# A Mamba-2 layer's chunk states: 32-bit products against three passes of 16-bit halves

## The reference, cut to what matters

```python
xdt = xc * dtc[..., None]
scores = einsum('bclhn,bcshn->bchls', Cc, Bc) * Lmat
Ydiag = einsum('bchls,bcshp->bclhp', scores, xdt)
decay_states = exp(cs[..., -1:] - cs)
states = einsum('bclhn,bchl,bclhp->bchpn', Bc, decay_states, xdt)   # the product that changes
new = carry * cd + st                                                # a recurrence over the chunks
Yoff = einsum('bclhn,bchpn,bchl->bclhp', Cc, prev, exp(cs))
y = (Ydiag + Yoff + x * D) * silu(gate); out = y * rsqrt(mean(y*y) + eps) * norm_w; out @ out_proj.T
```

## Time and profile before

| | |
|---|---|
| time before, median of 3 runs | 2475.66 us (2474.8 to 2475.94) |
| the profiled execution, its own time | 2476.66 us |
| span of its instructions | 2474.6 us |
| mean granted TensorE clock over the span | 0.984 of full speed |
| PE busy | 2373.2 us, 96% |
| DVE, ACT, POOL busy | 1791.4, 1591.7 and 1255.2 us |

### The profile page before, as it was taken

How to read it: one execution, slowest core, us unless ns; L and a number is a source line. 1 busy time by engine, 2 the same in 40 slices (tenths; PEclk the granted TensorE clock), 3 DMA queues, 4 the chain that set the end, 5 groups by cost and what they waited for, 6 DMA issues and landing times. The chain is left out here.

```text
span 2474.6 us, 48904 instructions
## 1 busy us (share of the span) xinstructions
PE 2373.2 (96%) x15424; PEld 1359.8 (55%) x15624; DVE 1791.4 (72%) x3234; ACT 1591.7 (64%) x3327; POOL 1255.2 (51%) x1002
## 2 busy tenths in 40 slices
PE   6999999999999999999999998789999999999897
PEld 3555555555555555555555555445555555555443
DVE  5677787787777777787777776577777777778522
ACT  7676776776776776776776775365556555656422
POOL 4465555555556556556556569443434343454223
PEclk8999999999999999999999999989999999999899
DMA  7343343343343343343343441320110110100000
GB/s 249 101 132 108 115 130 107 115 131 108 113 133 105 115 133 106 114 134 105 113 134 105 131 146 50 138 89 1 43 44 1 44 44 1 43 18 1 1 0 34
DMA packets 113827, 218.79 MB, mean 88 GB/s; under 512 B 9632, under 2 KB 43040, under 8 KB 111360
## 3 DMA queue, kind: packets, MB, share of 16 engines
q1 hardware_dynamic: 113536, 215.28, 27.0%
HBM read 212.10 MB, written 3.15 MB: 87 GB/s over the span
## 5 line engine op out<-in xcount | busy, mean ns | idle before, releaser
L989 ACT ACTIVATE E<-wq,cst 128x128 f32<-128x128 f32 x1024 | 311.7, 389 | 3.0 <-PEq L298 3.0
L256 DVE SCALAR_TENSOR_TENSOR xc<-bank,taps,xc 128x511 f32<-128x511 f32 (+2 forms) x384 | 284.9, 742 | 35.5 <-ACT xc L243 18.0
L1919 POOL TENSOR_TENSOR qT<-qT,qrot 128x512 f32<-128x512 f32 x64 | 81.2, 1269 | 370.1 <-DVE qrot L1809 370.1
L1282 POOL TENSOR_TENSOR acc<-acc,sq 128x512 f32<-128x512 f32 x112 | 173.1, 1545 | 183.3 <-ACT sq L1001 183.3
L1273 POOL TENSOR_TENSOR xw<-xt,wdec 128x384 f32<-128x384 f32 x128 | 106.4, 831 | 294.1 <-DVE xt L1124 150.7
L1166 DVE SCALAR_TENSOR_TENSOR u<-xc,D,bank 128x512 f32<-128x512 f32 x128 | 95.6, 747 | 205.8 <-PE bank L814 194.2
L1105 DVE TENSOR_TENSOR E<-E,cbm 128x1024 f32<-128x1024 f32 x128 | 242.8, 1897 | 0.8
L59 PE MATMUL bank<-xhi,wx 128*128 128x512 f16 x640 | 242.8, 379 | 0.0
L60 PE MATMUL bank<-xlo,wx 128*128 128x512 f16 x640 | 242.8, 379 | 0.0
L61 PE MATMUL bank<-xhi,wx 128*128 128x512 f16 x640 | 242.6, 379 | 0.0
L1268 POOL TENSOR_TENSOR ecs<-ecs,xcC 128x768 f32<-128x768 f32 x128 | 234.1, 1829 | 0.4 <-POOLq L298 0.4
(11 more groups left out here) (240 smaller groups left out, 6315.0 us busy)
## 6 DMA issues: line engine op xcount, KB each, us to landing
wq<-cs_rows SPq DMA_DIRECT2D x128, 512.0 KB, 4.1
ecs<-ecs_rows SPq DMA_DIRECT2D x128, 384.0 KB, 3.6
wx<-in_w_xbc SPq DMA_DIRECT2D x80, 256.0 KB, 2.7
wz<-in_w_z SPq DMA_DIRECT2D x64, 256.0 KB, 2.7
wo<-in_w_o SPq DMA_DIRECT2D x64, 256.0 KB, 4.0
wq<-in_wq SPq DMA_DIRECT2D x8, 1024.0 KB, 5.8
awo<-in_wo SPq DMA_DIRECT2D x8, 1024.0 KB, 5.0
wkv<-in_wkv SPq DMA_DIRECT2D x8, 512.0 KB, 3.9
```

What stands on the lines that cost most here:

```text
L256: self.nc.vector.scalar_tensor_tensor(out=dst[:, d:T], in0=self.k.bank[bank][:, 0:T - d], scalar=self.taps[:, bass.ds(g, 1), b, j, 3 - d:4 ...
L989: ins = nc.scalar.activation(E[t.i % 4][:, h, c], sc.csr[t.i % 2][:, h, c * P:(c + 1) * P], ACT.Relu, scale=-1.0, bias=head(sc.cst, t, c, h))
L1282: nc.gpsimd.tensor_tensor(acc[t.b][:], acc[t.b][:], sq[:], ALU.add).then_inc(acc_done, 1)
```

## The change

PE's chunk states are no longer three products of 32-bit words: each is three passes over 16-bit halves, in the same place of PE's list. The halves come from these places:

- `bt` becomes `bthi` (16-bit, written by ACT as before, with the semaphore `bt_hi`) and `btlo`, the remainder, a new instruction of DVE in slot i = 6 (`rest_of_B`, and once in the opening). PE's wait is now on DVE's semaphore.
- `xw` stays in 32 bits; its leading half is read in place by `lead`. Its remainder `xwlo` is a new instruction of POOL behind each `xw`. PE's wait is now on the semaphore of the remainder.
- On DVE `turned_x` moves from behind the third tap to ahead of it, wherever there are taps of x.
- On PE `turn_B` moves from behind `output` to ahead of it, in slot i = 6.

```diff
-        bt = [sb(f"bt{i}", [P, CH - 1, P]) for i in range(NB)]
+        bthi, btlo = ([sb(f"bt{n}{i}", [P, CH - 1, P], F16) for i in range(NB)] for n in ("hi", "lo"))
+        xwlo = [sb(f"xwlo{i}", [P, CH - 1, P], F16) for i in range(2)]
...
                 def states(t):
-                    pe.wait_ge(xw_done, t.n + 1)
+                    pe.wait_ge(xw_lo, t.n + 1)
                     pe.wait_ge(bt_done, t.u + 1)
                     for c in range(CH - 1):
-                        mm = nc.tensor.matmul(W[:, c * P:(c + 1) * P], bt[t.b][:, c], xw[t.i % 2][:, c], start=True, stop=True)
+                        mm = product(nc, W[:, c * P:(c + 1) * P], (bthi[t.b][:, c], btlo[t.b][:, c]),
+                                     (lead(xw[t.i % 2][:, c]), xwlo[t.i % 2][:, c]), True, True)
                     mm.then_inc(st_ready, 1)
...
+                    if nu and s.i == 6:
+                        turn_B(nu)
                     if tile_at(g, m - 1):
                         for half in range(2):
                             output(tile_at(g, m - 1), half)
                     if nu and s.i == 5:
                         products_CB(nu)
-                    if nu and s.i == 6:
-                        turn_B(nu)
...
+                def rest_of_B(t, bank):
+                    dve.wait_ge(bt_hi, t.u + 1)
+                    nc.vector.tensor_tensor(btlo[t.b][:], k.bank[bank][:, 0:(CH - 1) * P].rearrange("p (c n) -> p c n", n=P),
+                                            bthi[t.b][:], ALU.subtract).then_inc(bt_done, 1)
...
                     if n3:
-                        taps("x", sc.xc[n3.i % 4], n3, 2 + n3.i, (remainder, None))
+                        taps("x", sc.xc[n3.i % 4], n3, 2 + n3.i, (remainder, lambda: turned_x(n2)))
                     else:
                         remainder()
-                    if n2:
-                        turned_x(n2)
+                        if n2:
+                            turned_x(n2)
...
+                    if nu and s.i == 6:
+                        rest_of_B(nu, ring_bank(s.b, USE_BT))
...
                     pool.wait_ge(xt_done, t.n + 1)
                     nc.gpsimd.tensor_tensor(by_head(xw[t.i % 2][:]), by_head(xt[t.i % 2][:, 0:CH - 1]), of_heads(sc.wdec, t, 0, CH - 1),
                                             ALU.mult).then_inc(xw_done, 1)
+                    pool.wait_ge(xw_done, t.n + 1)
+                    x = xw[t.i % 2][:]
+                    nc.gpsimd.tensor_tensor(xwlo[t.i % 2][:], x, lead(x), ALU.subtract).then_inc(xw_lo, 1)
```

More of the change, by code:

```diff
@@ L658, in mixer @@
         out_half, cb_ready, bt_ready, ss_ready = S("out_half"), S("cb_ready"), S("bt_ready"), S("ss_ready")
-        clip_done, exp_done, sq_done, hi_done, gz_done, bt_done = S("clip_done"), S("exp_done"), S("sq_done"), S("hi_done"), S("gz_done"), S("bt_done")
+        clip_done, exp_done, sq_done, hi_done, gz_done, bt_hi = S("clip_done"), S("exp_done"), S("sq_done"), S("hi_done"), S("gz_done"), S("bt_hi")
         y_done, yg_done, s_step, m_done, xt_done = S("y_done"), S("yg_done"), S("s_step"), S("m_done"), S("xt_done")
@@ L666, in mixer @@
         cs_done, xw_done, acc_done, rstd_done = S("cs_done"), S("xw_done"), S("acc_done"), S("rstd_done")
-        acc_split = S("acc_split")
+        acc_split, xw_lo, bt_done = S("acc_split"), S("xw_lo"), S("bt_done")
         Y, W, OUT = k.bank[2], k.bank[3], k.bank[4:8]
@@ L1011, in turned_B @@
                     act.wait_ge(bt_ready, t.u + 1)
-                    nc.scalar.copy(bt[t.b][:], k.bank[bank][:, 0:(CH - 1) * P].rearrange("p (c n) -> p c n", n=P)).then_inc(bt_done, 1)
+                    nc.scalar.copy(bthi[t.b][:], k.bank[bank][:, 0:(CH - 1) * P].rearrange("p (c n) -> p c n", n=P)).then_inc(bt_hi, 1)
                 def first():
@@ L1155, in first @@
                     masked_CB(tile_at(0, 0), ring_bank(1, USE_CB))
+                    rest_of_B(tile_at(0, 0), ring_bank(1, USE_BT))
                     for c in range(CH - 1):
```

## The result

| | before | after |
|---|---|---|
| median, us (runs) | 2475.8 (2474.8 to 2478.32, 6) | 2454.97 (2454.11 to 2456.59, 6) |
| ratio to before | | 0.9915, 95% interval 0.9904 to 0.9926 |
| profiled execution: own time, span | 2476.66, 2474.6 | 2454.44, 2452.3 |
| mean granted TensorE clock | 0.984 | 0.985 |

The change makes the kernel 20.8 us faster (0.85%). The same kernel, measured once more in experiment 11, gave 2456.65 us (0.993, interval 0.9917 to 0.9944), so its gain is 18 to 21 us.

The account below looks back on a forecast made before the run. PE was taken to bound most loop slots, POOL the tail. Terms of -19.2 (states), +0.8 (`xwlo`), +0.4 (`btlo`) and +2.9 (tail) gave -15.1 us, a median of 2461 us; own range 2456 to 2466, 2455 to 2471 with the third rival.

Parts of the forecast that it names:

- What bounds the kernel: Mixer loop: PE, busy 307.7 of 310 us, bounds most slots; four slots wait for ACT's gate, POOL bounds the tail.
- PE's states: States of a tile: six passes at 0.672 us become nine at 0.509, saving 0.163 us a tile.
- The tiles that count: 128 tiles less four gate-bound slots and the last six leave 118 that save 0.163 us each, 19.2 us off.
- The wait for `xwlo`: Loop slots: POOL's remainder makes PE wait longer only in five second slots of an iteration, 0.8 us on.
- the long price: POOL's remainder held up by other work, in the tail another 0.75 us for each of four: 3 us, total 2464.
- `btlo` and the opening: DVE's remainder of B, 0.55 us, 16 times, is hidden except in the opening, where PE waits: 0.4 us on.
- The tail: Last tiles: POOL has no idle time, so its remainders delay the last two scans, 2.9 us on.
- The idle times ahead of the scans: PE's idle time ahead of the tail's last two scans grows from 4.76 and 2.90 us to 7.4 and 3.8.
- Loads that aren't hidden: Rival: nine state loads stand one behind the other, a tile takes 0.21 us more, total 2505 us; chance 6%.
- Waits for `xwlo` in most slots: Rival: the remainder takes 0.9 us more everywhere, 14 us of PE waits and 3.5 in the tail, 2478; chance 6%.
- ACT's chain in every second slot: Rival: ACT's gate holds every second slot, so 9.6 us of the saving stays in a wait, 2471; chance 8%.
- The move does nothing: Rival: `xt` waits for PE's transposes, so each `xwlo` is 0.9 us late; counted with the waits-for-`xwlo` rival.

Follow-up runs that it names:

- experiment 11: The changed kernel as it is, measured once more beside the version with the last four tiles' remainders on DVE: 2456.65 us, ratio 0.993.
- experiment 1: The kernel before with only the states' products as nine 16-bit passes on leading halves, no remainders and no new DVE or POOL instruction: 2452.58 us, ratio 0.9902.
- experiment 7: The kernel before with the third of the three 32-bit state products left out, four passes in place of six: 2481.0 us, one run.
- experiment 4: The changed kernel with a fourth pass in each state product, remainder by remainder, 12 passes a tile in place of nine: 2471.23 us, ratio 0.9981.
- experiment 3: The changed kernel with x times dt (`turned_x`) back behind the third tap on DVE: 2465.27 us, ratio 0.9956.
- experiment 6: The changed kernel with B's transposes back behind the output product in slot i = 6: 2455.56 us, ratio 0.9917.
- experiment 2: The kernel before with only POOL's remainder instruction behind each `xw`, read by nobody: 2479.35 us, ratio 1.0012.
- experiment 9: The kernel before with PE's two waits for the states (`xw`, `bt`) moved ahead of the scan and output product of the same slot: 2527.26 us, one run.
- experiment 10: The kernel before without the third 32-bit state product, plus 12 unused small products in PE's opening that shift the loop's code: 2450.71 us, one run.
- Experiment 12: The changed kernel with the last four tiles' remainders made by DVE instead of POOL, run beside the changed kernel: 2451.67 us, ratio 0.9906.

## Why the prediction came out as it did

**What bounds the kernel: right.** The windows show PE busy 308 of 310 us after, and the slots shortened by what PE's list lost.

**PE's states: the step that failed.** The prediction said: "From the first of their loads to the next load behind them it is 609.82 to 610.48, 0.66 us ... over all tiles the mean is 0.67, which I take", and so a saving of 0.163 us. The multiplications' own rows give 0.772 us for the six passes, and experiments 1 and 7 agree with it. The 0.10 us between comes from the lead that the load behind the states has (0.11 us), and the one at their start hasn't. Less 0.524 us for the nine passes (forecast 0.509) it is 0.248 us. The rest of the step stands: nine passes of 0.0566 us, confirmed by experiment 4. With 0.248 in the forecast's own term, 118 x 0.248 is 29.3 us, and its sum would have been -25.2 us. Up to the last scan the profile is in fact 24.6 us shorter. That the total came within 6 us of the forecast is in part luck: the 2.34 us that the rest of the program took longer stand in no term of the prediction, and they hide as much of its error.

**The tiles that count.** Slots up to the last five of the tail gave 27.5 us of the 30.3 that 122 full savings would be, so 2.8 us were lost at the starts of iterations. The prediction had about 1.8 (four slots lost whole, 1.0 us at 0.248 each, and 0.8 for waits). Both sorts of loss are the ones it named. Places 0 and 1 fall short of full savings by 2.0 us, and that part it had too small. The count of four slots was one of before. PE's waits for ACT's gate went from three to nine: with a shorter list PE comes to the gate sooner, in six of the eight slots in place 1. Some of them even grew, one from 10.8 to 11.6 us. Experiment 1 has seven such waits, experiment 4, with 12 passes, four. In place 0 six slots were already 0.1 to 0.7 us longer than PE's list before, and the prediction passed over them.

**The wait for `xwlo`: right in the loop.** Place 2 falls short of full savings by 0.7 us, the forecast had 0.8. The remainder takes 0.826 us (forecast 0.825), and in the loop PE waits for it only in place 2, the loop's second slot, six times; the prediction named that slot and five times. Three waits in the tail it hadn't named, so the waits are 3.9 us in all and not some 2. With the gate's nine waits there are eighteen, where the prediction took more than ten as a sign of being wrong. The 0.08 us between `xw` and `xwlo` is as forecast, though the taps that it was read from are 0.15 us apart. By the trace no `xwlo` ran beside a DVE instruction with both inputs in SBUF, so the long price of the prediction was never put to the test. Experiment 3 shows what stood on the move of `xt`: 9 to 10 us.

**`btlo` and the opening: right.** DVE takes 0.558 us (forecast 0.55). By the timeline PE's first states wait for it, and start 0.50 us later than in the earlier trace rows:

```profile
57.07 0.22 PE L59 MATMUL bank<-xw,bthi 128*128 128x128 bf16 x1 [4.03 <-DVE btlo L1136]
```

The first scan is 0.61 us later; the forecast was 0.4. In the other profiles with `btlo` it lies between 0.1 and 1.9 us later than in that of before, so the agreement is no proof of the term. The order of B's transposes changes nothing (experiment 6).

**The tail: right, a little large.** The last two slots are 1.89 and 0.89 us longer, together 2.78 (forecast 2.9; POOL's remainder alone 2.74 in experiment 2); the three slots ahead of them still saved 0.54 us, which the forecast had counted out. POOL's timeline shows the order that was described: the first `ecs` ends at 1496.45, the scan starts at 1496.55, and one `xwlo` more stands ahead of the next.

```profile
1494.65 1.80 POOL L1278 TENSOR_TENSOR ecs<-ecs,xcC 128x768 f32<-128x768 f32 x1
...
1498.54 0.82 POOL L1287 TENSOR_TENSOR xwlo<-xw 128x384 f16<-128x384 f32 x1
...
1509.94 1.80 POOL L1278 TENSOR_TENSOR ecs<-ecs,xcC 128x768 f32<-128x768 f32 x1
```

The idle times ahead of the scans were to be 7.4 and 3.8 us and are 5.67 and 2.88. PE's timeline shows why: part of the new idle time stands elsewhere in the same slots.

```profile
1484.14 0.23 PE L59 MATMUL bank<-xw,bthi 128*128 128x128 bf16 x1 [1.14 <-POOL xwlo L1287]
...
1496.55 1.12 PE L811 MATMUL bank<-E,xt 128*64 128x128 f32 x8 [5.67 <-issue]
...
1502.87 0.66 PE L1437 MATMUL bank<-identity,resid 128*128 128x128 f32 x4 [1.40 <-DVE xlo L1407]
...
1511.84 1.12 PE L811 MATMUL bank<-E,xt 128*64 128x128 f32 x8 [2.88 <-issue]
```

1.14 and 5.67 us make 6.8, 1.40 and 2.88 make 4.3. The stage's end is set by POOL in both kernels, so the slots' lengths are the measure, and the idle time ahead of one instruction is not.

**The rivals.** Loads that aren't hidden: no, steps are 0.0566 us. Waits for `xwlo` in most slots: not in the changed kernel, but that is what experiment 3 is, at a lower price than the rival's 14 us. ACT's chain in every second slot: no, only at the start of each iteration. The move does nothing: no, it is worth 9 to 10 us. The range's low end is given as 2455 in one place of the prediction and 2456 in another; the time lies below both.

**The stretch in no term.** From the last scan on nothing was changed, and yet that stretch took 2.34 us more in the profile of the result. Over the fourteen profiles it is 936.6 to 938.1 us where the states are 32-bit (before, experiments 2, 7, 9 and 10), and 939.3 to 941.1 us where they are 16-bit. The trace shows one place for most of it, a few us behind the jump back of the attention layer's own loop. PE's timeline there, before and after:

```profile
1971.34 0.38 PE L59 MATMUL bank<-xhi,wq 128*128 128x512 f16 x1
...
1947.03 0.39 PE L59 MATMUL bank<-xhi,wq 128*128 128x512 f16 x1 [2.00 <-issue]
```

PE stands still for 2.00 us with no releaser named. Then the granted clock is 0.55 of full speed from 1947.9 to 1951.0 us, near the lower of its two levels (1.2 of 2.4 GHz), and passes that were 0.22 us apart are 0.43 us apart. The stop, of 1.7 to 2.3 us, is in all eight profiles whose states are nine passes, and in none of the others. Experiment 4 doesn't have it, though its states are 16-bit too; its three more passes put the code behind them elsewhere (its 1.2 us more than before come in another place). So it looks like the stall of experiments 7 and 10 again, at another loop. Then most of the 2.34 us is a cost of where instructions lie; no experiment shifted them there by themselves.

**What stays open.** Why PE stops there is argued and not shown. Of the 32-bit states it stays open why their first load doesn't start early in the loop, where no wait stands ahead of it either (experiment 9). Experiment 12's total is 2.7 us lower against the changed kernel than its tail accounts for.

## What to carry to other kernels

Price a group of products from the start of its first MATMUL to the start of the next group's first, not from the loads, whose lead differs from group to group (here 0.67 us was read for 0.77). When a new operand has to be ready sooner by its own duration, look for a neighbour on the way that can be moved ahead by as much, and ask at the tail separately, where another engine may be the bound. Before blaming an edit for a per cent in a kernel with a hardware loop, look at the slot behind the jump back: here a change elsewhere in the program moved 30 us of 2480.

## What the runs showed of the hardware that was not expected

- The first of six 32-bit passes of 128 columns behind 64-column 32-bit products took 0.213 us, the others 0.112; the first of nine 16-bit passes at the same place 0.07, the others 0.0566. Where the first 32-bit load started 0.21 us ahead of its pass, the first step was 0.11.
- Two kernels that differ in 12 unused products ahead of the loop differ by 30 us, in one run each: six stalls of PE behind the jump back, 3.3 to 4.1 us of idle time each, and slots of 16 us instead of 11.
- A smaller stall stands behind each of the six jumps back. In the changed kernel DVE's `u` in place 1 waits 1.6 to 2.4 us in the six slots behind a jump, and the trace names no releaser. The same slot in the tail, with no jump ahead of it, has none. DVE's timeline shows the two kinds:

```profile
623.44 0.75 DVE L1174 SCALAR_TENSOR_TENSOR u<-xc,D,bank 128x512 f32<-128x512 f32 x1 [1.78 <-issue]
...
1350.45 0.73 DVE L1174 SCALAR_TENSOR_TENSOR u<-xc,D,bank 128x512 f32<-128x512 f32 x1
```

- A GpSimd instruction of 1.04 us makes a DVE one with two inputs in SBUF last 1.32 us instead of 0.68, or 1.44 instead of 0.74. Putting it elsewhere on POOL only chose another victim.
